# One graph layer with routed experts: the experts' segments without the extra product on TensorE

## The reference

```python
xf = x.reshape(-1, D)                      # x: normalised sum of the layers before, 6250 x 256
logits = xf @ router_w.T + router_b        # 32 experts
idx = jnp.argmax(logits, axis=-1)
h = jnp.einsum('nd,ndh->nh', xf, jnp.take(W1, idx, axis=0)) + jnp.take(b1, idx, axis=0)
h = jax.nn.relu(h)                         # 64 wide
out = jnp.einsum('nh,nhd->nd', h, jnp.take(W2, idx, axis=0)) + jnp.take(b2, idx, axis=0)
out = jax.nn.relu(out)
return x_in + out
```

## Time and profile before

| | us |
|---|---|
| median of 3 runs | 2876.47 |
| lowest and highest | 2868.52, 2883.56 |
| profiled execution | 2884.98 |
| its span, first to last instruction | 2883.2 |
| TensorE busy in the span | 2631.6 |
| GpSimd busy in the span | 1756.9 |

### The profile page before, as it was taken

How to read it: one execution, slowest core, us unless ns; L and a number is a source line. 1 busy time by engine, 2 the same in 40 slices (tenths; PEclk the granted TensorE clock), 3 DMA queues, 4 the chain that set the end, 5 groups by cost and what they waited for, 6 DMA issues and landing times.

```text
span 2883.2 us, 57776 instructions
## 1 busy us (share of the span) xinstructions
PE 2631.6 (91%) x19546; PEld 2462.9 (85%) x19546; DVE 2143.3 (74%) x4892; ACT 1581.4 (55%) x3080; POOL 1756.9 (61%) x1614
## 2 busy tenths in 40 slices
PE   5889999999989999998999999899999998993497
PEld 3667899999989999997999999799899998993365
DVE  8988677777767777776777777788888886894055
ACT  0545476666636666664666666444444445671165
POOL 2045587777778777777877776555555553224566
PEclk7999999999999999999999999999999998996699
DMA  6022322222242232224222222343333322201343
GB/s 127 29 49 55 96 64 68 64 58 61 51 116 60 61 69 59 64 45 118 60 64 64 65 59 51 94 120 89 86 89 87 93 75 57 62 26 39 83 116 94
DMA packets 255570, 207.99 MB, mean 72 GB/s; under 512 B 165506, under 2 KB 194387, under 8 KB 255278
## 3 DMA queue, kind: packets, MB, share of 16 engines
q1 hardware_dynamic: 197678, 162.55, 21.8%
q0 software_dynamic: 57600, 41.75, 7.3%
HBM read 136.93 MB, written 70.16 MB: 72 GB/s over the span
## 4 chain that ended last, share of the span: by engine, by line
PE 59%; DVE 15%; POOL 11%; issue 9%; ACT 2%; DVEq 1%; DMA 1%; SPq 0%; ACTq 0%; POOLq 0%; another core or an unknown queue 0%
PE bank L399 54%; POOL edges_sorted L787 7%; PE bank L1918 4%; DVE hidh_lo L1394 3%; POOL tokens_sorted L853 2%; DVE xh L1358 2%; DVE scr L1268 1%; DVE oh L1591 1%; DVEq L1570 1%; PE bank L2381 1%; POOL ehl L803 1%; DVE bn L1349 1%; POOL r L765 1%; DMA queries<-qn 1%; DVE res L1366 1%
## 5 line engine op out<-in xcount | busy, mean ns | idle before, releaser
L787 POOL DMA_INDIRECT edges_sorted<-staging,pos_i x850 | 1075.7, 1265 | 246.4 <-issue 229.8
L910 ACT ACTIVATE hid<-bank,b1p 128x250 f32<-128x250 f32 x800 | 331.5, 466 | 319.3 <-PE bank L399 286.3
L399 PE MATMUL bank<-w_hi,hidh_hi 128*125 128x256 f32 x1600 | 472.2, 295 | 23.1 <-DVE hidh_lo L1394 22.9
L399 PE MATMUL bank<-h_hi,w_hi 128*128 128x250 f32 x1600 | 479.1, 299 | 3.7 <-DVE h_lo L1378 3.4
L399 PE MATMUL bank<-w_hi,hidh_lo 128*125 128x256 f32 x1600 | 453.7, 284 | 0.0
L1394 DVE TENSOR_TENSOR hidh_lo<-hid,hidh_hi 128x500 fp32r<-128x500 f32 x400 | 319.7, 800 | 178.6 <-ACT hidh_hi L916 145.7
L399 PE MATMUL bank<-w_lo,hidh_hi 128*125 128x256 f32 x1600 | 452.2, 283 | 0.0
L399 PE MATMUL bank<-h_hi,w_lo 128*128 128x250 f32 x1600 | 448.5, 280 | 0.0
L399 PE MATMUL bank<-h_lo,w_hi 128*128 128x250 f32 x1600 | 445.0, 278 | 0.0
L399 PEld LDWEIGHTS bank<-w_hi,hidh_hi 128*125 128x125 f32 x1600 | 300.8, 188 | 32.1 <-DVE hidh_lo L1394 29.3
L399 PEld LDWEIGHTS bank<-h_hi,w_hi 128*128 128x128 f32 x1600 | 303.9, 190 | 8.4 <-DVE h_lo L1378 6.1
(11 more groups left out here) (292 smaller groups left out, 6625.5 us busy)
## 6 DMA issues: line engine op xcount, KB each, us to landing
staging<-edges_sorted SPq DMA_DIRECT2D x103, 260.0 KB
staging<-in_edge_attr SPq DMA_DIRECT2D x50, 531.2 KB
queries<-qn SPq DMA_DIRECT2D x100, 250.0 KB
qin<-queries SPq DMA_DIRECT2D x100, 250.0 KB
edges_sorted<-staging,pos_i POOLq DMA_INDIRECT x850
rows_in<-edges_sorted SPq DMA_DIRECT2D x50, 260.0 KB
yin<-tokens_sorted SPq DMA_DIRECT2D x81, 127.0 KB
raw<-in_L_mix_W SPq DMA_DIRECT2D x8, 1024.0 KB, 5.6
```

What stands on the lines that cost most here:

```text
L399: return nc.tensor.matmul(o, left, right, start=start, stop=stop, skip_group_check=True)
L787: nc.gpsimd.indirect_dma_start(out=edges_sorted, out_offset=bass.IndirectOffsetOnAxis(ap=pos_i[:, i:i + 1], axis=0), in_=stage[:, slot, j, ...
L910: a = nc.scalar.activation(hid[c % 2][:, j, :], chunks(PH[c % 2])[:, j, :], ACT.Gelu, bias=b1p[:, 2 * c + j:2 * c + j + 1])
```

## The change

The constant that says how many of the extra products stand at the end of each turn of TensorE's loop goes from one to none. The 48 products ahead of the loop stay.

```diff
 IDLE_SCATTER = 48
-IDLE_SEGMENT = 1
+IDLE_SEGMENT = 0
```

## The result

The changed kernel takes 2922.65 us (median of 4 runs, 2919.03 to 2936.81), the kernel before 2873.75 us in the same comparison: 1.0175 times as long, 95% interval 1.013 to 1.022. Forecast were 2925 us and "slower", by a granted clock that falls in the experts' stage and does not come back.

The account below looks back on a forecast made before the run. TensorE, busy 91% of the span, was taken as the bound, GpSimd just behind. Terms +48.3, -0.6 and -1.8 gave +46: 2931 us against the profiled execution, 2922 against the median; forecast 2925, range 2858 to 2942.

Parts of the forecast that it names:

- The price of the product: TensorE's turn in the experts' stage: 0.23 us less at full clock (to 1.37), 0.43 less at half (to 2.49).
- The clock: TensorE's granted clock in the experts' stage falls and stays down, or nearly, without the product; chance 0.58.
- The place of the fall: In the experts' stage, the clock falls at about 2723, as in the kernel before, where first rows came late.
- The sum: Whole span: the experts' stage's terms total +46 us, 2931 against the profiled execution, 2922 against the median.
- fifth to last transposes: Experts' stage, fifth to 81st pair of transposes: 76 turns at 2.49 us take 189.2 us instead of 140.9, +48.3.
- Behind the last transposes: End of the experts' stage: 13.0 us instead of 14.8, -1.8, as GpSimd has no arrears.
- the part ahead of them: Start of the experts' stage, ahead of the fifth transposes: three products fewer, at either clock, about -0.6 us.
- ScalarE's stalls: ScalarE's 2.6 us stalls in the experts' stage: put at nothing, since at half clock it can catch up.
- clock stays up: Rival: experts' stage at GpSimd's pace, 1.49 us a scatter; 25 us less, 2851 against the median; chance 0.16.
- Nothing changes: Rival: in the experts' stage TensorE's freed time becomes waits for ScalarE, turns keep their length: 2876 us; chance 0.08.

Follow-up runs that it names:

- the once-only burst: Kernel before, with no extra product in the turns but 16 in a row once, in turn 40 of 85: 2930.55 us, ratio 1.0129.
- the kernel with 128 rows: Changed kernel (no extra product), each segment's second product over all 128 array rows instead of 65: 2887.45 us, ratio 0.998 to the kernel before.

## Why the prediction was right

**The price of the product** was right at both clocks: 1.37 and 2.49 us a turn, with nothing in its place.

**The clock.** That it would fall and stay down was right, and the once-only burst and the kernel with 128 rows show that this, and nothing else in the turn, makes the loss. The reason given, that the product was the densest part of the turn, agrees with what the rows of the second product did. The place of the fall was not right: at 2746 instead of 2723. The first rows' delay did not bring the clock down; it fell 23 us later, behind three waits of which only the first is put down to ScalarE. 65 of the 76 turns behind the fifth transposes ran at the half clock.

**The sum** was +46 and is +40 by the spans (2923.2 against 2883.2). By its terms: fifth to last transposes 181.3 us (2727.4 to 2908.7) instead of 189.2, as eleven turns still ran at the full clock. Behind the last transposes 14.5 us instead of 13.0: the last four rows came faster than the 2.49 us of a full turn and GpSimd had arrears again, at 1.50 us a scatter, which the term had put at none. The stage began 2 us later (2721.3) and reached the fifth transposes at the same time, so the part ahead of them got 2 us shorter instead of 0.6, as the clock was still up there. Between the medians the loss is 49 us, since the profiled execution of before lay 11 us above its median. That 2925 was met within 3 us is in part luck: where the clock falls differs from one execution to the next (2746 and 2757), and the four runs go from 2919 to 2937.

**ScalarE's stalls** at nothing: right at the half clock, where TensorE has no gap in 128.00 us.

**The rival "clock stays up"** was wrong in its price, as far as the kernel with 128 rows can stand for it. With the clock up, that kernel gains 6 to 8 us, not 25: GpSimd's 1.49 us is a floor that the stage doesn't reach, as stalls whose cause is open, and to a small part SyncE's reads, keep the turn at 1.76 to 1.85 us. So a clock that stays up would have given "the same", and the chance of 0.14 for "faster" rested on a bound taken from the drain at the end of the stage, where nothing else was left to wait for.

**"Nothing changes"**: in the stretches at the full clock this rival was near the truth. From 2727.4 to 2746.8 eleven turns took 1.76 us each though TensorE needs 1.37; the freed time did turn into waits there, though not for ScalarE alone. The half clock then decided.

**The Trainium skill** (TensorE: Matmul & The Clock Gate, Part 1, "What's actually happening") has the full clock return after sustained activity. Here 162 us of work without a break, by the instructions' spans, did not return it: the measurement decides. The same section of the Trainium skill puts the cost of coming up to speed under 1% of a typical kernel's span. Here the loss was 1.3 and 1.75%, as the clock did not come up again at all.

## What to carry to other kernels

Before a product that nobody reads is taken out, look at the granted clock where it stands and at how long a fallen clock took to come back: if it comes back late even with the product, it may not come back without it, and every turn without waits then takes 1.8 times as long (2.49 us against 1.37 here). A few waits of under a microsecond then cost not a microsecond or two, but the rest of the stage at the lower clock. Better than an extra product is to let the work that is needed anyway use the whole array, where that costs no time: here a second product over 128 rows instead of 65 fetched the clock back within 3.4 us of each fall without adding to the turn.

## What the runs showed of the hardware

- TensorE at 1.2 GHz for 162 us (changed kernel) and 270 us (64-row product, one outlying execution), busy without a gap in both.
- The same turn with a second product over 128 rows instead of 65: still 2.49 us at the half clock and 1.37 at the full one, but half-clock spells of 3.4 us (14 of 15 in five kernels' traces; the other was 6.8) where with 65 rows the clock did not come back.
- An extra product of half the rows or half the columns makes the turn longer than a full one does: 3.51 us against 2.92 at the half clock with 64 rows, 1.93 against 1.60 at the full clock with 64 columns. With the first product padded from 64 to 128 columns the turn without waits is 0.17 us shorter (1.20 for 1.37).
- An extra product of 64 moving columns costs a turn as much as one of 128 (1.60 us).
